# Expert routing counted into slots in phase one, with rows scattered there and results gathered in phase three

## The reference, cut to what matters

```python
scores = softmax(xf @ gate_w.T)                   # xf: 4096 tokens x 128
_, idx = top_k(scores + gate_b, 6)                # 6 experts of 64 per token
weights = take_along_axis(scores, idx)
# an expert keeps its first 64 tokens (CAP); pos = a token's place in its expert
xb[expert, pos] = xf[token]                       # 64 x 64 rows
h  = silu(xb @ w1.T) * (xb @ w3.T)                # 64 x 64 x 88
yb = h @ w2.T                                     # 64 x 64 x 128
y[token] += yb[expert, pos] * weights             # nothing for dropped pairs
z  = silu(xf @ ws1.T) * (xf @ ws3.T) @ ws2.T      # shared expert, every token
x  = layernorm(xf + y + z)
```

## Time and profile before

| what | value |
|---|---|
| median of 3 runs | 2058.49 us (2055.42 to 2058.86) |
| the profiled execution's own time | 2058.53 us |
| its span, first to last instruction | 2056.7 us |
| PE busy | 1732.1 us, 84% of the span |
| DVE busy | 1123.0 us, 55% |
| ACT busy | 894.7 us, 44% |
| POOL busy | 230.6 us, 11% |
| mean granted TensorE clock | 0.913 of full |

### The profile page before, as it was taken

How to read it: one execution, slowest core, us unless ns; L and a number is a source line. 1 busy time by engine, 2 the same in 40 slices (tenths; PEclk the granted TensorE clock), 3 DMA queues, 4 the chain that set the end, 5 groups by cost and what they waited for, 6 DMA issues and landing times.

```text
span 2056.7 us, 47809 instructions
## 1 busy us (share of the span) xinstructions
PE 1732.1 (84%) x19224; PEld 1120.0 (54%) x19224; DVE 1123.0 (55%) x2308; ACT 894.7 (44%) x1641; POOL 230.6 (11%) x392
## 2 busy tenths in 40 slices
PE   3778777887769599799889889989979988988995
PEld 1444444444468457456556655655745655665663
DVE  5567667666664453653663563465364366356343
ACT  2444454444322244544454354544454445435452
POOL 0000010001046200100100010010010010001000
PEclk9889898878779799899899999989999999989997
DMA  7300000000075500000000010010000000000000
GB/s 280 133 22 24 24 13 19 20 23 8 13 157 81 160 12 3 22 22 3 19 25 3 2 42 3 3 39 5 3 22 22 4 19 25 2 3 6 1 2 6
DMA packets 51259, 66.43 MB, mean 32 GB/s; under 512 B 6599, under 2 KB 41905, under 8 KB 50243
## 3 DMA queue, kind: packets, MB, share of 16 engines
q1 hardware_dynamic: 47971, 60.23, 9.0%
q0 software_dynamic: 2560, 3.46, 1.8%
q10 hardware_dynamic: 576, 0.39, 0.1%
HBM read 41.73 MB, written 24.12 MB: 32 GB/s over the span
## 4 chain that ended last, share of the span: by engine, by line
PE 70%; DVE 12%; ACT 8%; issue 5%; DMA 2%; POOL 1%; SPq 0%; ACTq 0%; DVEq 0%; POOLq 0%; PEldq 0%
PE psum L568 7%; PE psum L833 6%; PE psum L940 6%; PE psum L731 5%; DVE peak L1218 4%; PE psum L581 3%; PE psum L820 3%; ACT prob L1095 3%; PE psum L893 3%; PE psum L791 3%; PE psum L593 3%; PE psum L726 2%; PE psum L630 2%; PE psum L637 2%; PE psum L866 2%
## 5 line engine op out<-in xcount | busy, mean ns | idle before, releaser
L1095 ACT ACTIVATE prob<-psum 128x1024 f32<-128x1024 f32 (+2 forms) x384 | 339.9, 916 | 281.5 <-PE psum L720 97.5
L1218 DVE TENSOR_REDUCE w_shared<-psum 128x4 bf16<-128x1024 f32 x128 | 155.4, 1226 | 166.1 <-PE psum L637 166.1
L1218 DVE TENSOR_REDUCE peak<-psum 128x4 bf16<-128x1024 f32 (+2 forms) x176 | 210.2, 1219 | 63.1 <-PE psum L677 29.6
L1388 POOL TENSOR_TENSOR rstd<-moments,eps 128x2 f32<-128x2 f32 x80 | 15.6, 195 | 1382.6 <-DVE moments L1136 1382.6
L833 PE MATMUL psum<-prob,v_big 128*64 128x256 f32 x1024 | 129.9, 398 | 18.3 <-issue 18.2
L940 PE MATMUL psum<-w_late,qt 128*128 128x128 f32 x1024 | 139.9, 298 | 1.3 <-DVE qt L1247 1.3
L940 PEld LDWEIGHTS psum<-w_late,qt 128*128 128x128 f32 x1024 | 131.6, 210 | 15.4 <-issue 15.0
L568 PE MATMUL psum<-xt,w_late 128*128 128x256 f32 x512 | 133.6, 405 | 5.6 <-ACT xt L1014 4.7
L731 PE MATMUL psum<-qt,kt 64*128 64x256 f32 x1024 | 131.4, 376 | 0.0
L1201 DVE TENSOR_REDUCE w_shared<-psum 128x8 bf16<-128x512 f32 x64 | 41.3, 688 | 142.4 <-PE psum L644 142.0
L568 PEld LDWEIGHTS psum<-xt,w_late 128*128 128x128 f32 x512 | 93.2, 196 | 37.7 <-issue 12.3
(11 more groups left out here) (262 smaller groups left out, 3123.5 us busy)
## 6 DMA issues: line engine op xcount, KB each, us to landing
zd<-kx SPq DMA_DIRECT2D x24, 512.0 KB, 5.3
union<-zd SPq DMA_DIRECT2D x16, 768.0 KB, 4.5
xg<-union SPq DMA_DIRECT2D x16, 192.0 KB, 2.0
w_late<-in_w1T SPq DMA_DIRECT2D x1, 2816.0 KB, 12.6
kt<-in_w2T SPq DMA_DIRECT2D x4, 704.0 KB
union<-in_x SPq DMA_DIRECT2D x16, 128.0 KB, 2.2
union<-in_xT SPq DMA_DIRECT2D x16, 128.0 KB, 2.2
xtd<-x_out SPq DMA_DIRECT2D x16, 128.0 KB, 1.8
```

The source lines that it names most:

```text
L1095: nc.scalar.activation(prob[s][:, slot + 2 * i:slot + 2 * i + 2, 0:n], v.pair(step, i)[:, :, 0:n], ACT.Exp, scale=a.scale).then_inc(v.free ...
L1218: nc.vector.tensor_reduce(dst, src, axis=AX.X, op=ALU.max).then_inc(v.free(step), 1)
```

## The change

**Phase one.** The lists are gone. `next_slot` holds, for each of the 64 experts, the next free slot in `xe`, a DRAM buffer of 64 x 64 rows. R2 is now a matrix product of the mask with a strict triangle and with ones, which counts earlier tokens of the same expert; R3 adds the counts to `next_slot`, zeroes what is past capacity and takes the 8 greatest, which gives six row numbers per token (4096, which is out of bounds, for a dropped pair). Twelve new steps RS per sequence, on POOL, each scatter 128 token rows by an index DMA straight to `xe`; RW waits on POOL until all twelve have landed. The row numbers are kept in DRAM (`places`).

**Middle part.** "merge", "slots", and POOL's gathers and scatters are gone. SP loads each chunk's rows whole from `xe` and stores the results whole to `ye`. In UP the tokens are now the stationary operand, which leaves the hidden layer with tokens on the partitions, so a new step HT transposes it back (four transposes and a copy on ScalarE, twice a chunk); UP has two PSUM banks in place of three. Of the shared expert's halves 19 come ahead of chunk 0 (12 before) and 3 stand in each chunk (5 before). Two of the wide weights are loaded after the third chunk's UP, the others after the fourth's.

**Phase three.** Twelve new steps G per sequence, on POOL, each gather 128 result rows of 128 values from `ye`, in place of the one whole load. `TURNS` and `AHEAD` are new for both phases.

```diff
@@ streams
-                        + ([("RL", "R", s, i) for i in range(4)] if s == 1 else []))
+                        + [("RS", "R", s, i) for i in range(2 * TOPK)] + [("RW", "R", s, 0)])
-    front = lambda s: [("Z", "F", s, 0), ("Y", "F", s, 0), ("L", "F", s, 0), ("XT", L1, s, 0)]
+    front = lambda s: [("G", "F", s, i) for i in range(2 * TOPK)] + [("Z", "F", s, 0), ...]
-AHEAD1, AHEAD3 = (33, 26, 0, 0), (27, 13, 4, 4)
+AHEAD1, AHEAD3 = (35, 29, 0, 0), (20, 8, 16, 16)
...
@@ vector_step, R3
+                linked(tt(slot, counts, next_slot.unsqueeze(1).to_broadcast(spread), ALU.add))
+                tt(next_slot, next_slot, v.bank(step)[:, 2 * E:3 * E], ALU.add).then_inc(y.slots_moved, 1)
+                linked(tt(left, slot, past_slot.unsqueeze(1).to_broadcast(spread), ALU.is_lt))
...
+                linked(tt(left, left, slot, ALU.mult))
+                linked(tt(left, left, r_mask[s][:, :, :], ALU.mult))
+                for t in range(2):
+                    last = nc.vector.max(r_top[s][:, t, :], left[:, t, :])
...
@@ pool_step
+            if kind == "RS":
+                t, k = step[3] // TOPK, step[3] % TOPK
+                if step[3] == 0:
+                    pool.wait_ge(y.r_placed[s], v.once())
...
+                pool.indirect_dma_start(
+                    out=xe[:, :], out_offset=bass.IndirectOffsetOnAxis(
+                        ap=r_place[s][:, step[3]:step[3] + 1].bitcast(U32), axis=0),
+                    in_=xs[s][:, t, :], in_offset=None, bounds_check=E * CAP - 1, oob_is_err=False,
+                ).then_inc(y.rows_out[s], 16)
+            if kind == "RW":
+                pool.wait_ge(y.rows_out[s], v.at(32 * TOPK, 32 * TOPK))
+                pool.sem_inc(y.rows_done[s], 1)
+            if kind == "G":
...
+                pool.indirect_dma_start(
+                    out=routed[s][:, t, k, :], out_offset=None, in_=ye[:, :],
...
@@ expert_steps
-            out = [("merge", 0), ("F1", 0), ("F1", 1), ("slots", 0)] + shared(10)
+            out = [("F1", 0), ("F1", 1)] + shared(17)
             for c in range(CHUNKS):
-                out += [("XT", c, 0)] + shared(1) + [("XT", c, 1)] + shared(1) + [("UP", c)] + shared(1)
-                out += [("DOWN", c, 0)] + shared(1) + [("DOWN", c, 1)] + shared(1)
+                out += [("XT", c, 0), ("XT", c, 1)] + shared(1) + [("UP", c)] + shared(1) + [("HT", c, 0), ("HT", c, 1)]
+                out += shared(1) + [("DOWN", c, 0), ("DOWN", c, 1)]
@@ experts_transfers
+            for q in AB:
+                sp.wait_ge(p1.rows_out[q], ITERS * 32 * TOPK)
+            for c in range(CHUNKS):
+                sp.dma_start(e_x[c], xe[1024 * c:1024 * c + 1024, :].rearrange("(n p) w -> p n w", p=128)).then_inc(
+                    e_x_in[c], 16)
...
-                elif kind == "UP" and c == CHUNKS - 1:
-                    sp.wait_ge(e_h_full, 4 * CHUNKS)
-                    for dst, name in wide3:
+                elif kind == "UP" and c >= CHUNKS - 2:
+
+                    sp.wait_ge(e_h_full, 4 * c + 4)
+                    for dst, name in wide3[:2] if c == CHUNKS - 2 else wide3[2:]:
...
+                if kind == "DOWN" and step[2] == 1:
+                    sp.wait_ge(e_y_ready, 2 * c + 2)
+                    sp.dma_start(ye[1024 * c:1024 * c + 1024, :].rearrange("(n p) d -> p n d", p=128), e_y[c]).then_inc(
+                        stored, 16)
...
@@ pool
-            experts_pool(pool)
             pool.wait_ge(p3_ready, 1)
+            pool.wait_ge(stored, 16 * CHUNKS)
```

More of the change, by code:

```diff
@@ L19 @@
 EPS = 1e-5
-ROUNDS = CAP // 8
 XW = D + E
@@ L162, in fills @@
         return ["Q"]
-    if kind in ("D", "L", "C", "CK", "RN", "RL", "Z", "Y") or kind == "W" and step[3]:
+    if kind in ("D", "L", "C", "CK", "RN", "R3", "RS", "RW", "G", "Z", "Y") or kind == "W" and step[3]:
         return []
@@ L1122, in scalar_step @@
                 last.then_inc(v.free(step), 1)
-            elif kind == "R2":
-                act.wait_ge(*v.filled(step))
-                copy(r_maskt[s][halves[s], :], v.bank(step)[halves[s], 0:256]).then_inc(v.free(step), 1)
         def layer_norm_sums(dve, v, s, which, src):
@@ L1316, in vector_step @@
             elif kind == "R3":
-                dve.wait_ge(*v.filled(step))
-                rows = halves[s]
-                new = key_list[rows, CAP:CAP + T]
-                dve.wait_ge(y.sorted, v.at(2 * ROUNDS, 1))
-                dve.wait_ge(y.key_moved[s], v.once())
-                dve.wait_ge(zeroed, 24 * 16)
-                tt(new, v.bank(step)[rows, 0:256], token_key[rows, :], ALU.add).then_inc(v.free(step), 1)
-                dve.wait_ge(*v.drained(step))
-                tt(new, new, r_maskt[s][rows, :], ALU.mult).then_inc(y.r_keyed[s], 1)
@@ L1503, in decoder_program @@
         w2_in = [sem(f"w2_in{p}") for p in AB]
-        gathered = [sem(f"gathered{c}") for c in range(CHUNKS)]
-        scattered = sem("scattered")
+        e_x_in = [sem(f"e_x_in{c}") for c in range(CHUNKS)]
+        stored = sem("stored")
         e_xt_full = sem("e_xt_full")
@@ L1581, in experts_tensor @@
                     for n in range(4):
-                        last = mm(psum[:, XT_BANK, n * 128:n * 128 + 128], e_x[c][:, 4 * step[2] + n, 0:D], ident[:, :],
-                                  start=True, stop=True)
+                        last = nc.tensor.transpose(psum[:, XT_BANK, n * 128:n * 128 + 128], e_x[c][:, 4 * step[2] + n, 0:D],
+                                                   ident[:, :])
                     last.then_inc(e_xt_full, 1)
@@ new lines, in experts_scalar @@
+                        h1 = psum[:, UP_BANKS[pair % 2], 0:4 * FI].rearrange("p (n k f) -> p n k f", n=2, k=2)[:, :, 0, :]
+                        nc.scalar.activation(e_h[c % 2][:, 2 * q:2 * q + 2, :], h1, ACT.Tanh, scale=0.5).then_inc(e_act, 1)
+                elif kind == "HT":
+                    part = 2 * c + step[2]
+                    act.wait_ge(e_ht_full, part + 1)
+                    if part >= 2:
+                        act.wait_ge(e_y_full, part - 1)
+                    nc.scalar.copy(e_ht[step[2]], psum[0:FI, HT_BANK, :]).then_inc(e_ht_ready, 1)
```

304 lines of the change are left out of this document (132 added, 172 removed).

## The result

The changed kernel takes 2094.95 us (median of 4 runs, 2091.19 to 2104.38) against 2057.48 us; the ratio is 1.019, with a 95% interval of 1.0151 to 1.0229. The profiled execution took 2091.19 us, its span is 2089.4 us, 32.7 us more than before's. The prediction had the sign right (slower, 0.53), its 2067.1 us has a quarter of the real loss (8.6 us of 37.5), and the time lies 3 us above its range, which ended at 2092.

The account below looks back on a forecast made before the run. Phase three was taken as bound by TensorE's work, phase one and the middle part by chains of engines waiting for each other. Sum: 2058.5 - 10.0 + 1.0 + 17.0 + 0.6 = 2067.1 us, range 2032 to 2092.

Parts of the forecast that it names:

- slower, 0.53: Whole kernel: predicted sign of the change, slower 0.53, against same 0.10 and faster 0.37.
- Phase one was forecast at -10.0 us: Phase one: net gain of 1.25 us per iteration, eight times, from less sorting minus `rstd` waits behind scatters.
- The sort's 1.85 us per iteration: Phase one: the sort delays VectorE twice in A's chain, 0.83 and 1.02 us; removing it gains 1.85 us per iteration.
- "Durations as before" for the new order: Phase three's loop: TensorE's work unchanged, gathers run ahead; 0 us taken for the new order.
- The bounds of -8 and +12: Phase three's loop: limits in us around the 0 taken for the new order.
- Scatters on the path: 0.6 us per iteration: Phase one: an `rstd` meets at most the scatter under way, 0.3 us; two in A's chain make 0.6.
- The rival "POOL becomes the bound": Phase one: if each scatter took 1.74 us, POOL comes near 65 us per iteration; 2093 us in all, chance 0.09.
- The middle part: Last mask to last copy: 1 us lost, bounds -8 and +10, two old waits exchanged for a new one.
- stall: Middle part: ScalarE's third copy waits 13.5 us for the shared expert's first store, queued behind scatters and loads.
- The opening: Last copy to phase three's first transpose: 17.0 us lost, with six loads, then thirteen gathers on POOL taking 16.3 us.

Follow-up runs that it names:

- e11: Changed kernel with all scatters and gathers left out (POOL raises the semaphores), order kept: 2044.9 us against 2059.6 us for the kernel before.
- e7: Kernel before with the sort's work left out of phase one's loop, order unchanged: 2059.4 us against 2059.9 us for the kernel before.
- e6: Kernel before with the changed kernel's order of phase three alone, without its gathers' turns: 2083.9 us, 0.9872 of the kernel before.
- e14: Kernel before with the new order of phase three and two wide weights loaded after the third chunk's UP: 2020.3 us, 0.9805 of the kernel before.
- e12: Changed kernel with the old order of attention steps in phase one, a scatter behind every second step: 2136.8 us against 2059.6 us for the kernel before.
- e9: Changed kernel with each scatter replaced by a plain DMA from POOL's queue to fixed rows: 2077.5 us against 2059.9 us for the kernel before.
- e10: Changed kernel with every second scatter left out and waits halved to match: 2094.8 us against 2059.9 us for the kernel before.
- e4: Changed kernel with SyncE's last-scatter wait and expert-row loads behind the shared expert's fifth to eighth stores: 2213.3 us against 2111.9 us for the kernel before.
- e13: Changed kernel with expert-row loads behind the shared expert's fifth to eighth stores, places and contexts loaded early: 2078.0 us, 1.010 of the kernel before.
- e8: Changed kernel with phase three's 192 gathers left out (POOL raises the semaphore), order kept: 2062.1 us against 2059.9 us for the kernel before.
- e5: Changed kernel with expert-row loads moved later on SyncE, places and contexts loaded early, on another chip: 2207.7 us against 2112.3 us for the kernel before.
- e2: Changed kernel with its 192 scatters left out (POOL raises the semaphore), all orders kept: 2133.7 us against 2111.9 us for the kernel before.
- r1: Kernel before, no edit, traced on a further chip beside the changed kernel: 2109.2 us.
- r2: Changed kernel, no edit, on a further chip: 2239.2 us against 2112.3 us for the kernel before.

## Why the prediction was wrong

Phase one was forecast at -10.0 us, -14.8 for the sort and +4.8 for the scatters, with all else as before. Measured is +23.7. Without any index DMA the last mask already came 13.1 us later than before (e11), and the scatters bring the other 10.6. So 28 us of the miss lie in the gain that didn't come and in the order and contents taken as neutral, and 6 us in the price of the scatters. In the other direction phase three was forecast at +0.6 and came out at -15.2.

**The sort's 1.85 us per iteration** is the step that failed first. I had read two rows in which VectorE came late to a transpose, and taken both delays for a gain of the whole iteration. e7 measured none, though both delays were gone in its trace. So they weren't the bound of the loop: closing them moved waits to other places. Which ones wasn't followed. In e7 TensorE was busy 315.0 us in six iterations at a mean clock of 0.84, in before 312.1 us at 0.86, so a part of what was won may have gone to the clock; that isn't shown.

**"Durations as before" for the new order** is the second step. I had costed the contents and taken M, the tail and phase three's loop over from before's trace. e11, free of all index DMAs, shows what the new order does together with the new router: iterations 0.6 to 0.9 us longer, and the last mask 13 us later. Most of that is the tail: A's and B's last masks lie 13.9 us apart (566.1 and 580.0), before 4.2, so B's router ends alone. How the 0.6 to 0.9 us divide between the order and the new R2 and R3 wasn't parted. Phase three is 22 us shorter than before's 1351.5 (1329.1), and there e6 and e14 show with the old content that it is the order. The bounds of -8 and +12 that I gave phase three did not hold it.

**Scatters on the path: 0.6 us per iteration** was right for what it named: against e11 VectorE waited 0.6 us longer for `rstd` per iteration. But the scatters cost 2.2 us in all (e11 against the changed kernel), and the term had nothing beside the `rstd` waits. What stands beside them in the trace is TensorE at a lower granted clock, with 1.8 us more of busy time per iteration. One iteration of the changed kernel, cut where its clock changes, and the 2 us ahead of the second fall:

```profile
193.00:197.00 4.00, 3.42 (x52) 2.62 (x52) 2.48 (x8) 0.48 (x1) 0.21 (x2) 0.57 0.04 12
197.00:217.00 20.00, 15.02 (x251) 9.25 (x241) 9.59 (x38) 11.11 (x25) 14.08 (x16) 1.00 0.05 10
217.00:242.00 25.00, 19.84 (x171) 10.02 (x171) 14.97 (x34) 7.62 (x20) 12.14 (x13) 0.59 0.05 14
...
215.00:217.00 2.00, 0.60 (x4) 0.20 (x2) 1.31 (x7) 0.02 (x1) 1.29 (x3) 1.00 0.01 0
```

If the clock is at one of its two levels all the time, the means over six iterations (before and e11 0.86, the changed kernel 0.82) make an estimated 18, 19 and 25 us of each iteration at the lower one. In e12 a gap of 4.5 us was followed by 15 us at the lower level, and here the clock fell behind 2 us in which TensorE was busy for 0.60. But that the clock is the cause of the remaining 1.6 us isn't shown. TensorE's busy time doesn't set the iteration by itself: e9's was 4.3 us shorter than e11's for the same stretch. And of the 11 us that e10's six iterations are longer than e11's, 5.1 are busy time and 3.2 `rstd` waits. So the sum of the scatters' price is measured, and its division stays open. The Trainium skill (page "TensorE: Matmul & The Clock Gate", section "What's actually happening") says that an array without enough work gets 1.2 GHz and that work brings 2.4 back; the rows of e12 agree with both levels, 0.50 behind the gap and 0.97 later.

**The rival "POOL becomes the bound"** gave 2093 us, two from the measured time, for a reason that did not occur: one scatter per iteration took 1.6 to 1.8 us, the others stayed near 0.97. That nearness is an accident.

**The middle part.** Right in kind, with sizes that are off in part: stall 20.7 for 13.5, copy +3.7 for +1.0. The stall ended 3.6 us later than forecast, the shared expert behind it took 20.0 us for 18, and from the first XT to the last copy it was 65.7 us for 68.5, as the first three chunks took 15.0 us each (661.48 to 676.48 between copies) for the 16.1 that I took. e4 and e13 show that the stall was a matter of the place in SyncE's queue: 16 and 14 us came back.

**The opening.** Right, 20.5 for 17.0, and e8 shows that it is the gathers. e5 and e13 take 5 to 6 us of it back by loading the places early (8 to 9 were expected); the rest is POOL's 16 us for thirteen gathers.

**What stays open.** Why on two chips index DMAs hold up the other engines. e2 and e4 show on one chip that the scatters are what does it (66.5 against 82.8 us), and r1 and r2 that either kernel pays where it uses them. Whether plain DMAs from POOL's queue would do it there too isn't known, as e9 ran on a chip without the effect. Instructions fetched by DMA would be one way: the Trainium skill (page "Runtime: NRT & Kernel Launch", section "Instruction fetch mechanics") says that each engine's sequencer fetches its code over a DMA queue of its own. The DMA view of r2 for an iteration of phase one speaks against it, since it lists no queue of kind instruction:

```profile
q1 hardware_dynamic: 1632, 0.90, 3.7%
q0 software_dynamic: 1152, 0.03, 0.9%
```

## What to carry to other kernels

Where a change comes with a new order of steps, cost the order by itself: run the old content in the new order, or the new order with the new work left out, before any edit is called a gain. Before's phase three went from 1359.5 to 1326.5 us by its order alone (r1, e6). Work taken from an engine that is 65% busy may be worth nothing, even where rows show that engine late: e7 closed two such delays and won nothing. Look also at the clock behind a hole in TensorE's stream: behind e12's, of 4.5 us, it was low for 15 us. A kernel that moves to index DMAs should be timed on several chips, with the kernel before beside it each time.

## What the runs showed of the hardware

- A difference between chips that depends on the program: before took 2057 us in the first runs, 2060 us on one further chip and 2112 us on two others, the changed kernel 2095 and 2239 us. Nearly all of it lies in stretches with index DMAs: before's middle part took 138.1 and 188.0 us (first trace and r1), its phase one 65.6 and 65.8 us per iteration, its phase three 1351.5 and 1359.5 us, where e7 on a chip without the effect had 1357.4.
- A plain DMA from POOL's queue holds POOL for 0.54 us (e9, median of 192), an index DMA of the same rows for 0.97 us with 0.30 behind it.
- Scatters landed 2.1 us after their issue (median of the changed kernel's 192), where the middle part of before had 4.7 for its own.
